# Layer-norm stage on two engines: ScalarE takes half of the normalisations, SyncE takes the stores

## The reference, cut to what matters

```python
def _layernorm(x, axis=-1, eps=1e-05):
    m = jnp.mean(x, axis=axis, keepdims=True)
    v = jnp.var(x, axis=axis, keepdims=True)
    return (x - m) / jnp.sqrt(v + eps)

x = x + _L0_attn_a_ref(_layernorm(x, axis=-1), ...)   # selective scan
x = x + _L0_ffn_ref(_layernorm(x, axis=-1), ...)
x = x + _L0_attn_b_ref(_layernorm(x, axis=-1), ...)   # long convolution
x = x + _L0_ffn_ref(_layernorm(x, axis=-1), ...)
```

## Time and profile before

| | us |
|---|---|
| median of 3 runs | 4691.2 (4690.49 to 4694.54) |
| profiled execution | 4688.05 |
| its span | 4686.3 |
| first stage, start to the next block's first transfer | 126.2 |
| mean granted TensorE clock | 0.959 |

### The profile page before, as it was taken

How to read it: one execution, slowest core, us unless ns; L and a number is a source line. 1 busy time by engine, 2 the same in 40 slices (tenths; PEclk the granted TensorE clock), 3 DMA queues, 4 the chain that set the end, 5 groups by cost and what they waited for, 6 DMA issues and landing times. The chain is left out here.

```text
span 4686.3 us, 118726 instructions
## 1 busy us (share of the span) xinstructions
PE 4287.6 (91%) x39924; PEld 3567.5 (76%) x39924; DVE 3240.8 (69%) x6737; ACT 2158.3 (46%) x5046; POOL 2370.2 (51%) x3284
## 2 busy tenths in 40 slices
PE   5399999999999999999999999999959999989999
PEld 3177777777777777777777777777738888878888
DVE  8766666666677666667666676666645666658888
ACT  3244444444444444444444444444426666645555
POOL 3275666665666665666565666565610000016666
PEclk9699999999999999999999999999979999999999
DMA  8311111111111111111111111111127666633333
GB/s 274 134 50 36 35 37 42 40 37 43 37 37 46 36 37 46 34 37 48 36 35 46 34 38 48 35 37 43 32 53 191 183 183 181 183 110 106 105 105 95
DMA packets 369775, 347.50 MB, mean 74 GB/s; under 512 B 24954, under 2 KB 343290, under 8 KB 360186
## 3 DMA queue, kind: packets, MB, share of 16 engines
q1 hardware_dynamic: 352380, 323.98, 23.3%
q10 hardware_dynamic: 16896, 16.78, 1.1%
HBM read 232.01 MB, written 108.66 MB: 73 GB/s over the span
## 5 line engine op out<-in xcount | busy, mean ns | idle before, releaser
L721 PE MATMUL bank<-w_bc,xnT 128*128 128x512 f32 x3072 | 814.7, 408 | 10.7 <-POOL xnT L1042 10.7
L924 ACT COPY turned_t<-bank 128x512 f32<-128x512 f32 x512 | 299.9, 586 | 857.5 <-PE bank L744 857.4
L721 PEld LDWEIGHTS bank<-w_bc,xnT 128*128 128x128 f32 x3072 | 569.5, 192 | 149.9 <-issue 35.3
L1050 POOL TENSOR_TENSOR steps<-upto,par 128x512 fp32r<-128x512 f32 x512 | 551.0, 1097 | 6.2 <-PE bank L730 6.2
L1455 PE MATMUL p_yc<-sig,toep 64*64 64x256 f32 (+14 forms) x16384 | 539.6, 282 | 15.2 <-issue 11.9
L1455 PEld LDWEIGHTS p_yc<-sig,toep 64*64 64x64 f32 x16384 | 476.0, 132 | 91.0 <-issue 44.5
L1159 DVE TENSOR_TENSOR rot<-bank,par 128x512 f32<-128x512 f32 x512 | 350.0, 684 | 247.1 <-PE bank L721 165.5
L1059 POOL TENSOR_TENSOR turned_b<-rot 128x512 f32<-128x512 f32 x256 | 325.3, 1271 | 306.5 <-DVE rot L1160 306.1
L754 PEld LDWEIGHTS bank<-turned_t 128*128 128x128 f32 x2048 | 300.7, 214 | 127.8 <-issue 105.3
L754 PE MATMUL bank<-turned_t 128*128 128x128 f32 x2048 | 309.5, 300 | 93.9 <-issue 92.3
L1179 DVE TENSOR_TENSOR mix<-bank,decay 128x512 f32<-128x512 f32 x256 | 175.6, 686 | 298.5 <-PE bank L754 297.9
(11 more groups left out here) (264 smaller groups left out, 9727.3 us busy)
## 6 DMA issues: line engine op xcount, KB each, us to landing
toep<-taps_dram SPq DMA_DIRECT2D x256, 260.0 KB, 4.2
el<-el_dram SPq DMA_DIRECT2D x256, 128.0 KB, 3.1
xg<-arg_x SPq DMA_DIRECT2D x32, 512.0 KB, 4.9
xnT_dram<-xt_g ACTq DMA_DIRECT2D x32, 512.0 KB, 4.2
xnT_raw<-xnT_dram SPq DMA_DIRECT2D x128, 128.0 KB, 2.5
x_quad<-arg_x SPq DMA_DIRECT2D x32, 512.0 KB, 3.9
x_dram<-x_quad SPq DMA_DIRECT2D x32, 512.0 KB, 3.8
x0T_dram<-conv SPq DMA_DIRECT2D x32, 512.0 KB, 2.8
```

The lines of the kernel that those rows point to most:

```text
L721: last = mm(p_bc[c][:, :], xnT[w.q % 2][p][:, k, :], w_bc[q][:, k, c * 1024 + g * W4:c * 1024 + (g + 1) * W4], start=(n == 0), stop=(n == ...
L924: s_.copy(turned_t[g][c][:, :], p_tr[:, :]).then_inc(s[f"copy_{BC[c]}"], 1)
L1050: last = g_.tensor_tensor(heads(steps[p][:, :]), upto[:, :].unsqueeze(1).broadcast_to([128, GROUP, TOK]), over(of_group(P_A + p * HEADS, w ...
```

## The change

ScalarE takes two of the four normalisations of every group, as activations with one scale and one shift per token; the scale is the reciprocal root, the shift minus the mean times it. GpSimd works out the shift: it multiplies the means by -1 and, behind a drain, by the reciprocal roots, before it signals `rstd_ready`. `xn_ready` is split into `front_ready` (VectorE's half) and `back_ready` (ScalarE's half), and whoever waited for it waits for both. Ahead of its statistics VectorE now waits for the reciprocal roots of two groups before; that wait stood ahead of the epsilon.

ScalarE's order in step i is now: normalise group i-1, copy group i-2, rows of group i-3. The store is no longer ScalarE's: SyncE issues it in the same queue as the loads, in step i the load of group i and then the store of group i-3, which waits for `xt_ready`. SyncE also takes over the closing wait for the stores.

```diff
--- before.py
+++ after.py
@@ -55,12 +55,13 @@
     two = lambda name, shape: [sb(f"{name}{p}", shape) for p in range(2)]
     xn, stats, mean_var = two("xn_g", [128, 4, DIM]), two("stats_g", [128, 4, 6]), two("mean_var_g", [128, 4, 2])
     var_eps, rstd, xt = two("var_eps_g", [128, 4]), two("rstd_g", [128, 4]), two("xt_g", [128, 4, KT, TOK])
+    minus_one, minus_mean, shift = sb("minus_one_g", [128, 4]), two("minus_mean_g", [128, 4]), two("shift_g", [128, 4])
     p_tr = [[ps(f"p_tr{p}{k}", [128, 4 * TOK]) for k in range(KT)] for p in range(2)]
     p_scT, scT = [ps(f"p_scT{p}", [128, TOK]) for p in range(2)], two("scT_g", [128, TOK])
     p_sc = [ps(f"p_sc{p}", [128, 4, 32]) for p in range(2)]
     x_in = [sem(f"x_in{k}") for k in range(R)]
     w_in, consts = sem("w_in"), sem("consts")
-    var_ready, rstd_ready, xn_ready = sem("var_ready"), sem("rstd_ready"), sem("xn_ready")
+    var_ready, rstd_ready, front_ready, back_ready = sem("var_ready"), sem("rstd_ready"), sem("front_ready"), sem("back_ready")
     transposed, xt_ready, scal_ready, scal_taken = sem("transposed"), sem("xt_ready"), sem("scal_ready"), sem("scal_taken")
     rows_ready, rows_taken = sem("rows_ready"), sem("rows_taken")
     xt_out = [sem(f"xt_out{p}") for p in range(2)]
@@ -89,10 +90,22 @@
             sp.dma_start(w_scal[:, :, 0:24], t["w_scal"].rearrange("(k p) n -> p k n", p=128)).then_inc(w_in, 16)
 
             def load(n, g, v):
-                wait(sp, xn_ready, n - R + 1)
+                wait(sp, front_ready, n - R + 1)
+                wait(sp, back_ready, n - R + 1)
                 sp.dma_start(xg[v % R][:, :, :], t["x"][bass.ds(n * 4 * TOK, 4 * TOK), :]
                              .rearrange("(q p) c -> p q c", p=128)).then_inc(x_in[v % R], 16)
-            rounds(sp, lambda on: on(0, load))
+
+            def store(n, g, v):
+                wait(sp, xt_ready, n + 1)
+                sp.dma_start(t["xnT_dram"][bass.ds(n * 4, 4)].rearrange("q p k t -> p q k t"),
+                             xt[v % 2][:, :, :, :]).then_inc(xt_out[v % 2], 16)
+
+            def body(on):
+                on(0, load)
+                on(3, store)
+            rounds(sp, body)
+            for p in range(2):
+                sp.wait_ge(xt_out[p], 16 * GROUPS // 2)
 
         @block.gpsimd
         def _(pool):
@@ -105,6 +118,7 @@
             g_.memset(t["wrap"][:, :], 0.0)
             g_.memset(t["minus_half"][:, :], -0.5)
             g_.memset(w_scal[:, :, :], 0.0)
+            g_.memset(minus_one[:, :], -1.0)
             pool.drain().then_inc(consts, 1)
             g_.affine_select(out=t["ident"][:, :], in_=t["ident"][:, :], compare_op=ALU.not_equal, fill=1.0,
                              base=0, pattern=[[-1, 128]], channel_multiplier=1)
@@ -128,8 +142,13 @@
 
             def token_rstd(n, g, v):
                 wait(pool, var_ready, n + 1)
-                wait(pool, xn_ready, n - 1)
-                g_.tensor_tensor(rstd[v % 2][:, :], var_eps[v % 2][:, :], t["minus_half"][:, 0:4], ALU.pow).then_inc(rstd_ready, 1)
+                wait(pool, front_ready, n - 1)
+                wait(pool, back_ready, n - 1)
+                p = v % 2
+                g_.tensor_tensor(rstd[p][:, :], var_eps[p][:, :], t["minus_half"][:, 0:4], ALU.pow)
+                g_.tensor_tensor(minus_mean[p][:, :], mean_var[p][:, :, 0], minus_one[:, :], ALU.mult)
+                pool.drain()
+                g_.tensor_tensor(shift[p][:, :], minus_mean[p][:, :], rstd[p][:, :], ALU.mult).then_inc(rstd_ready, 1)
             rounds(pool, lambda on: on(0, token_rstd))
 
         @block.vector
@@ -138,6 +157,7 @@
 
             def statistics(n, g, v):
                 p = v % 2
+                wait(dve, rstd_ready, n - 1)
                 wait(dve, x_in[v % R], 16 * (g + (v // R) + 1))
                 for q in range(4):
                     v_.bn_stats(stats[p][:, q, :], xg[v % R][:, q, :])
@@ -145,17 +165,16 @@
                 for q in range(4):
                     v_.bn_aggr(mean_var[p][:, q, :], stats[p][:, q, :])
                 dve.drain()
-                wait(dve, rstd_ready, n - 1)
                 v_.tensor_scalar(var_eps[p][:, :], mean_var[p][:, :, 1], LN_EPS, None, ALU.add).then_inc(var_ready, 1)
 
             def normalise(n, g, v):
                 p = v % 2
                 wait(dve, rstd_ready, n + 1)
                 wait(dve, transposed, n - 1)
-                for q in range(4):
+                for q in range(2):
                     last = v_.tensor_scalar(xn[p][:, q, :], xg[v % R][:, q, :], mean_var[p][:, q, 0:1], rstd[p][:, q:q + 1],
                                             ALU.subtract, ALU.mult)
-                last.then_inc(xn_ready, 1)
+                last.then_inc(front_ready, 1)
 
             def take_scalars(n, g, v):
                 wait(dve, scal_ready, n + 1)
@@ -174,7 +193,8 @@
 
             def transpose(n, g, v):
                 p = v % 2
-                wait(pe, xn_ready, n + 1)
+                wait(pe, front_ready, n + 1)
+                wait(pe, back_ready, n + 1)
                 wait(pe, xt_ready, n - 1)
                 for k in range(KT):
                     for q in range(4):
@@ -206,7 +226,15 @@
 
         @block.scalar
         def _(act):
-            def copy_and_store(n, g, v):
+            def normalise(n, g, v):
+                p = v % 2
+                wait(act, rstd_ready, n + 1)
+                wait(act, transposed, n - 1)
+                for q in range(2, 4):
+                    last = nc.scalar.activation(xn[p][:, q, :], xg[v % R][:, q, :], ACT.Identity, scale=rstd[p][:, q:q + 1], bias=shift[p][:, q:q + 1])
+                last.then_inc(back_ready, 1)
+
+            def copy_xT(n, g, v):
                 p = v % 2
                 wait(act, transposed, n + 1)
                 wait(act, rows_ready, n - 1)
@@ -214,9 +242,7 @@
                 for k in range(KT):
                     last = nc.scalar.copy(xt[p][:, :, k, :], p_tr[p][k][:, :].rearrange("p (q t) -> p q t", q=4))
                 last.then_inc(xt_ready, 1)
-                wait(act, xt_ready, n + 1)
-                act.dma_start(t["xnT_dram"][bass.ds(n * 4, 4)].rearrange("q p k t -> p q k t"),
-                              xt[p][:, :, :, :]).then_inc(xt_out[p], 16)
+
             def take_rows(n, g, v):
                 p = v % 2
                 wait(act, rows_ready, n + 1)
@@ -224,11 +250,10 @@
                 nc.scalar.copy(scT[p][:, :], p_scT[p][:, :]).then_inc(rows_taken, 1)
 
             def body(on):
-                on(1, copy_and_store)
-                on(2, take_rows)
+                on(1, normalise)
+                on(2, copy_xT)
+                on(3, take_rows)
             rounds(act, body)
-            for p in range(2):
-                act.wait_ge(xt_out[p], 16 * GROUPS // 2)
 
 
 def scan_and_filter(nc, ctx, t):
```

## The result

| | before | after |
|---|---|---|
| median of 18 runs each, us | 4691.4 (4680.1 to 4695.1) | 4681.7 (4675.7 to 4689.8) |
| ratio after to before | | 0.9982 (95%: 0.9974 to 0.9989) |
| profiled execution, its span | 4688.05, 4686.3 | 4679.71, 4677.6 |
| first stage: start to the next block's first transfer | 126.2 | 134.5 (+8.3) |
| from there to the mixer's first matmul | 114.9 | 114.4 (-0.5) |

The forecast was +2.6 us, and 4688 to 4702 us the range. The kernel became 9.8 us shorter at the median. It did not do so in the stage that was edited: this one lost 8.3 us, more than the forecast's 2.6, and a stage in which no line was edited gave back 14.3. The runs of one kernel spread over 14 to 15 us, and the rows from a trace are of one execution each, so a single row can be some us off by chance; the 8.3 us of the stage are not in doubt, the 14.3 need other runs beside them.

The account below looks back on a forecast made before the run. VectorE bounds the first stage now; after the change, loads held behind stores on SyncE's queue would. Seven terms sum to c = 10.9 us for three groups, ten turns give +2.6 us on 4691.2: 4693.8 us, range 4688 to 4702.

Parts of the forecast that it names:

- What bounds the kernel now: First stage: VectorE's order of work sets it, at 3.57 us a group; the stage lasts 126.2 us.
- ceiling: First stage: DMA engines' 0.97 share is a true limit, time stays 4691 to 4695; together with the forecast 0.72.
- Nothing outside it is edited; whatever it loses or gains is passed on one to one: Later stages start when the first stage's last store has landed, so its change reaches the total in full.
- a change in a later stage: Listed sign of a wrong forecast: any later stage changing by more than a few us.
- The loop c: First stage, statistics of group n+1 to those of n+4: 10.9 us for three groups, 3.63 a group.
- The landing: Loop's last term: a load on SyncE's queue lands 4.2 us after issue, ends 3.9 and 4.9.
- the load pays for the store in front of it: Rival, SyncE's queue: landing takes 4.9 us, c is 11.6, time +9.6 us, 4700.8; chance 0.17.
- The start and the end: First stage: statistics 1 begin at 8.6 us; from statistics 31 to the next block 10.8 to 11.2 us.
- ScalarE and GpSimd: First stage: ScalarE's two normalisations and two copies take 2.09 us, GpSimd's power to shift 1.55; both have room.
- VectorE stays the bound: Rival, first stage: loads not caught in the loop, 2.92 us a group, 20 us less, 4671; chance 0.03.
- The Trainium skill's fit: Transfer time of 2.0 us plus bytes at 436 GB/s, 3.2 us here; c would be 9.9, time 7.4 under before.

Follow-up runs that it names:

- store_lag4: The changed kernel with SyncE's store issued one step later in the same queue as the loads; 4661.6 us, ratio 0.9940.
- delay7: The kernel before with seven copies and drains added at the end of ScalarE's first stage, delaying the next block; 4697.2 us, ratio 1.0015.
- act_stores: The changed kernel with the store issued by ScalarE behind its copies, as before; 4664.8 us, ratio 0.9943.

## Why the prediction was wrong

**What bounds the kernel now: right** for the first stage. VectorE's order set it: with two normalisations of four left out (before_half) the next block came 10.8 us earlier, and the "ceiling" of the DMA engines at 0.97 was none, as 333 GB/s in store_lag4 show against 296.

**"Nothing outside it is edited; whatever it loses or gains is passed on one to one": this step failed**, and with it the sign. The first half is true of the text, the second of delay7, where 7.9 us later became 9.3 us longer (1.4 to 12.2). It is not true of an edit that changes the number of VectorE's instructions: there the mixer's 14.3 us outweigh the stage's 8.3. What the runs show instead is that the place of VectorE's recurring loss sets part of the mixer's time, shown for about 8 of the 18 us won behind the stage; the cause of the other 10 stays open. That the total fell is therefore luck of the program's layout and no merit of the change, which made its own stage slower: after_lead15, the same change behind 15 idle instructions, gains nothing. The prediction named a change in a later stage as what would make it wrong, but gave it no chance and no price. The rows of before would have allowed a bound: its rounds take 99.0 to 102.3 us with the same instructions in each, by how long TensorE is at the lower clock.

**The loop c: right as a mechanism, one term mis-sized.** Predicted 10.9 us for three groups, measured 11.5. Of the seven terms six hold within 0.1 us (2.17 to the power, 1.55 for the shift, 0.1, 2.09, 0.17; the issue of the load 0.65 where I had 0.6). The landing was taken at 4.2 and measured 4.7 at the median, 4.76 on average over loads 4 to 31 (counted from 0): that is 0.56 of the missing 0.6. I had reasoned that a load lands 1.5 us behind the store ahead of it, as the second of two loads does. Measured over the same 28 loads both parts are longer: the store ahead takes 3.7 us on average (3.2 to 4.7) where I had a lone one's 2.9, and the load lands 1.8 behind it (1.4 to 2.3). For example, the store issued at 65.74 takes 3.2 and is there at 68.9, the load issued at 66.39 takes 4.5 and is there at 70.9. Ten turns by 0.6 are the 6 us between 117.6 and 123.74. This is the rival "the load pays for the store in front of it", with c = 11.6; it had 0.17, and was right in its size (+8.3 in the stage against +9.6). That the store in the same queue is the reason isn't isolated: with the store on the other queue the loads took as long or longer, 4.9 in before and 5.2 in act_stores.

**The start and the end: right.** Statistics 1 begin at 8.63 us (8.6), and from statistics 31 to the next block are 10.8 us (10.8 to 11.2).

**ScalarE and GpSimd: right.** Two normalisations and two copies 2.05 us (2.09), power to the shift's end 1.52 (1.55); neither is a bound. The added waits of VectorE and GpSimd cost nothing.

**"VectorE stays the bound" at 2.92 us a group: wrong in its size.** With the loop opened the stage runs at 3.16 to 3.29; what holds VectorE then is other waits (`p_sc` in act_stores, loads and the shift in store_lag4).

**The Trainium skill's fit** (page "DMA: Bandwidth & Descriptors", section "Anatomy of one DMA — SWDGE (gpsimd) path"), an estimate of 3.2 us for a transfer, would have made c 9.9; the measured landings start at 4.2.

## What to carry to other kernels

Before a store moves into a queue of loads, write down what it waits for and at which step that is done: in the same place of the queue it cost 15 us, one step later it gained. Time the whole kernel, but judge an edit by the milestones of its own stage: two variants of this kernel differ by 8 us through 17 instructions that do nothing, so a difference of 0.2% in the total says little on the edit itself. To separate the two, add idle instructions ahead to the better variant and to the worse; of store_lag4's 26.3 us only half lies in the edited stage (13.5 us), the other half in stages of which no line was edited.

## What the runs showed of the hardware that was not expected

- VectorE loses about 0.35 us once in every 128 instructions of a long straight program; the place moves with the number of instructions that stand ahead in the text, and comes back to the same places of the round of 224 when 32 are added.
- At these places a DMA packet of 8192 bytes brings instructions (53 of 54 in before); TensorE's packets are of 16384 bytes, one for 256 instructions.
- In the mixer's rounds TensorE's slow stretches lasted 3.4 us, or twice that, at a granted clock of 0.50 (1.2 GHz), and each 3.4 us of them cost about 1.6 us of a round (99.0, 100.6 and 102.3 us with 3.4, 6.8 and 10.2 us of it).
- Before the slow stretch that begins at 707.5 us of after_lead15, TensorE had been busy 4.3 of 7.0 us; before the one at 758.7 us, 4.9 of 7.0.
- A load of 512 KB behind a store of 512 KB in one queue, issued 0.65 us later at the median, lands in 4.2 to 5.6 us, median 4.7, against 3.9 alone.
- One queue carried both directions at 333 GB/s, with the DMA engines at a share of 1.02.
